# Fetching one gather chunk of every 7th block row by row on SyncE, instead of every 14th

## The reference, cut to what matters

```python
# layer 0: messages
h_nodes = mlp2(x, ...)                                   # per node
msgs = mlp2(concat(h_nodes[dst], h_nodes[src], h_edges)) # per edge
x = x + layernorm(x + upd(segment_mean(msgs, dst)))      # per node
# layer 1: attention, 4 heads of 32
h = x @ W
alpha = segment_softmax(leaky_relu(a_src[src] + a_dst[dst]), dst)
out = x + segment_sum(h[src] * alpha, dst) + bias
```

## Time and profile before

| | us |
|---|---|
| median of 3 runs | 4091.2 (4089.45 to 4092.23) |
| the profiled execution | 4091.22 |
| its span, first to last instruction | 4089.1 |
| GpSimd busy | 2965.8 (73%) |
| PE busy | 3382.9 (83%) |
| first and last gather of the message pass start at | 112.1 and 2056.0 |
| first and last gather of attention start at | 2109.8 and 4053.1 |

### The profile page before, as it was taken

The page is one execution under the profiler, slowest core; times in us unless marked ns, Lnnn a source line. Parts: engine busy times, 40 slices in busy tenths (PEclk is TensorE's granted clock), DMA queues, the critical chain, the costliest instruction groups (busy, mean ns, idle before and its releaser), DMA issues. The chain is left out here.

```text
span 4089.1 us, 126775 instructions
## 1 busy us (share of the span) xinstructions
PE 3382.9 (83%) x30848; PEld 2976.2 (73%) x30849; DVE 2517.0 (62%) x10511; ACT 2850.5 (70%) x5940; POOL 2965.8 (73%) x3134
## 2 busy tenths in 40 slices
PE   7789888999988899999947777777777778777777
PEld 4677777777777788888847777777777767766776
DVE  5752222222222256777748777777777777888888
ACT  6466565656556577788738777777777777877777
POOL 2677777777777777777737777777777777777774
PEclk8789999999899899999967777777777777777777
DMA  5322222222222233333342222222222222332332
GB/s 159 88 60 53 54 55 53 56 53 53 55 54 53 60 83 91 91 96 95 81 120 58 57 58 58 57 58 58 58 57 58 58 58 63 79 78 76 78 78 58
DMA packets 319769, 282.90 MB, mean 69 GB/s; under 512 B 143418, under 2 KB 242924, under 8 KB 319532
## 3 DMA queue, kind: packets, MB, share of 16 engines
q0 software_dynamic: 99456, 159.33, 15.9%
q1 hardware_dynamic: 139224, 79.62, 7.4%
q10 hardware_dynamic: 80852, 41.75, 3.5%
HBM read 249.58 MB, written 29.40 MB: 68 GB/s over the span
## 5 line engine op out<-in xcount | busy, mean ns | idle before, releaser
L541 POOL DMA_INDIRECT a_G<-Htab,idx x1554 | 1470.8, 946 | 526.3 <-issue 464.0
L541 POOL DMA_INDIRECT p_rows<-Btab,idx x1554 | 1471.4, 947 | 475.1 <-issue 473.4
L1799 PE MATMUL a_psA<-a_GP,a_S 128*128 128x132 f32 x4704 | 892.5, 365 | 2.7 <-DVE a_GP L1634 2.7
L1799 PEld LDWEIGHTS a_psA<-a_GP,a_S 128*128 128x128 f32 x4704 | 821.5, 268 | 8.2 <-DVE a_GP L1634 3.1
L1056 DVE TENSOR_TENSOR p_z<-p_psZ,p_rows 128x512 f32<-128x512 f32 x294 | 195.9, 689 | 829.4 <-SPq L746 679.6
L1206 ACT COPY p_ST<-p_psT 128x1024 bf16<-128x1024 bf16 x294 | 300.5, 1022 | 563.7 <-PE p_psT L1318 543.4
L1730 ACT CAST a_S<-a_Sb 128x512 f32<-128x512 bf16 x588 | 608.6, 1144 | 0.0
L1365 PE MATMUL p_psA<-p_msg,p_S 128*128 128x65 f32 x4704 | 589.9, 284 | 10.9 <-ACT p_S L1227 9.8
L1365 PEld LDWEIGHTS p_psA<-p_msg,p_S 128*128 128x128 f32 x4704 | 571.6, 201 | 16.5 <-issue 12.8
L1227 ACT CAST p_S<-p_Sb 128x1024 f32 (+1 forms) x294 | 582.6, 1982 | 0.0
L1341 PEld LDWEIGHTS p_psZ<-wc,p_s 128*128 128x128 f32 x2352 | 325.1, 206 | 204.7 <-issue 103.5
(11 more groups left out here) (212 smaller groups left out, 5165.8 us busy)
## 6 DMA issues: line engine op xcount, KB each, us to landing
arena<-in_ea SPq DMA_DIRECT2D x196, 256.0 KB
p_single<-Btab SPq DMA_DIRECT2D x1792, 0.2 KB
a_single<-Htab SPq DMA_DIRECT2D x1792, 0.5 KB
p_rows<-Btab,idx POOLq DMA_INDIRECT x1554
a_G<-Htab,idx POOLq DMA_INDIRECT x1554
Htab<-u_H ACTq DMA_DIRECT2D x49, 136.0 KB
arena<-Htab SPq DMA_DIRECT2D x7, 952.0 KB
n_x<-in_x SPq DMA_DIRECT2D x14, 448.0 KB, 4.0
```

The source lines that it names most:

```text
L541: pool.indirect_dma_start(out=rows[:, u * C + c, :], out_offset=None, in_=table, in_offset=bass.IndirectOffsetOnAxis(ap=idx[u][:, c:c + 1] ...
L1799: m = pe.matmul(psA[v][:, 0:HR], S32[v][:, c, :], GP[v][:, c, :], start=c == 0, stop=c == C - 1)
```

## The change

SyncE takes the eighth chunk of the last block of every round of 7 blocks, the first round excepted, instead of every 14. That makes 27 such chunks in each pass instead of 14. GpSimd issues 7 x 28 x 8 - 27 = 1,541 indirect DMAs in each pass instead of 1,554. The row DMAs of SyncE go from 1,792 to 3,456 in each pass. They are fetched one round ahead into a doubled spare tile, in seven batches of 12, 20, 20, 20, 20, 16 and 20 rows, one after each block's `ready`.

The node numbers are turned into byte offsets once, in the opening: ACT loads them, DVE multiplies them by 256 and by 544, and SyncE stores both tables to HBM (`offsets`). The row DMA then reads a flat byte view of the table at the offset in the register. The source indices of GpSimd come as one DMA for 7 blocks, no longer as one DMA for each block. The tile `flagt` moves onto the storage of `x1`, with one wait on DVE at row NORM.

```diff
-BATCH = (12, 12, 12, 8, 12, 8, 12, 8, 12, 8, 12, 12)
+BATCH = (12, 20, 20, 20, 20, 16, 20)
+ROUNDS = NB // SLOTS
...
+            sp.wait_ge(s_off, 18)
+            for n in range(2):
+                sp.dma_start(offsets[n], bytes_[n][:, :]).then_inc(s_off, 16)
+            sp.wait_ge(s_off, 50)
...
+            act.dma_start(nodes[:, :], t["single"]).then_inc(s_off, 16)
...
+                dve.wait_ge(s_off, 16)
+                for n, size in enumerate((4 * H, 4 * HROW)):
+                    dve.tensor_scalar(bytes_[n][:, :], nodes[:, :], size, None, ALU.mult).then_inc(s_off, 1)
...
-        for c in range(C - 1 if odd and u == SLOTS - 1 else C):
+        for c in range(C if whole or u < SLOTS - 1 else C - 1):
+            at = u * C + c
             pool.indirect_dma_start(
-                out=rows[:, u * C + c, :], out_offset=None, in_=table,
-                in_offset=bass.IndirectOffsetOnAxis(ap=idx[u][:, c:c + 1], axis=0)).then_inc(s_g[u], 16)
+                out=rows[:, at, :], out_offset=None, in_=table,
+                in_offset=bass.IndirectOffsetOnAxis(ap=idx[odd][:, at:at + 1], axis=0)).then_inc(s_g[u], 16)
...
+        at = self.nc.values_load_multi_w_load_instructions(
+            self.k["at"][0:1, odd * P + first:odd * P + first + BATCH[n]], engines=[sp.engine], min_val=0,
+            max_val=(NP - 1) * self.size, skip_runtime_bounds_check_because="offsets of nodes")[1]
         for p in range(BATCH[n]):
-            sp.dma_start(self.spare[first + p:first + p + 1, :], self.table[bass.ds(which[p], 1), :]
-                         ).then_inc(self.s_row[n % 3], 16)
+            sp.dma_start(self.spare[first + p:first + p + 1, odd, :].bitcast(U8),
+                         self.table[bass.ds(at[p], self.size)].unsqueeze(0)).then_inc(self.s_row[n % 6], 16)
...
+    def landed(self, i):
+        for n in range(6):
+            self.sp.wait_ge(self.s_row[n], 16 * sum(BATCH[n::6]) * (i + self.before))
+            self.sp.sem_inc(self.s_turn, 1)
+
+    def step(self, i, odd, u, first, final):
+        if not first and u == 0:
+            self.landed(i)
+        if not first and u == SLOTS - 2:
+            self.place(i, odd)
+        if not final:
+            self.batch(i + 1, 1 - odd, u)
+            if u == 0 and not (isinstance(i, int) and i + 2 >= ROUNDS):
+                self.load(i + 2, odd)
...
-            load_idx(u if final else (i + 1) * SLOTS + u, u)
-            step_singles(singles, r, odd * SLOTS + u, final)
+            if u == 0:
+                load_idx(sp, t, k, 0 if final else i + 1, 1 - odd)
+            singles.step(i, odd, u, first, final)
```

More of the change, by code:

```diff
@@ L63 @@
 BOUNDED = "build_steps cuts blocks and windows off at their last"
-assert W == NG * GW and NG % 2 == 0 and NS % 2 == 0 and NB % SPAN == 0 and sum(BATCH) == P and len(BATCH) < SPAN
+assert W == NG * GW and NG % 2 == 0 and NS % 2 == 0 and NB % SPAN == 0 and sum(BATCH) == P and len(BATCH) == SLOTS
 assert 2 * MEAN - 6 >= NB - 1 and 2 * MEAN - 201 + 195 >= NB
@@ L138, in build @@
         k["mcur"], k["adst"] = k["attn"][:, :, 0:NH], k["attn"][:, :, NH:2 * NH]
[L141 to L145, removed]
+        k["at"] = sb("at", [1, 2 * P], I32)
+        k["singles"] = [sem("at"), [sem(f"row{n}") for n in range(6)], sem("to")]
+        k["slots"] = [[sem(f"src{u}") for u in range(2)]] + [[sem(f"{n}{u}") for u in range(SLOTS)] for n in ("rows", "side")]
+        k["idx"] = [sb(f"idx{u}", [P, SLOTS * C], I32) for u in range(2)]
         with ExitStack() as ctx:
-            opening(nc, t, k, hTkeep, Btab, lambda *a: sb(*a, ctx=ctx), sem, ctx)
+            opening(nc, t, k, hTkeep, Btab, offsets, lambda *a: sb(*a, ctx=ctx), sem, ctx)
         with ExitStack() as ctx:
-            message_pass(nc, t, k, Btab, Htab, hTkeep, x1keep, flagrows, lambda *a: sb(*a, ctx=ctx), sem, ctx)
+            message_pass(nc, t, k, Btab, Htab, hTkeep, x1keep, flagrows, offsets, lambda *a: sb(*a, ctx=ctx), sem, ctx)
         with ExitStack() as ctx:
-            attention_pass(nc, t, k, Htab, flagrows, x1keep, out, lambda *a: sb(*a, ctx=ctx), sem, ctx)
+            attention_pass(nc, t, k, Htab, flagrows, offsets, x1keep, out, lambda *a: sb(*a, ctx=ctx), sem, ctx)
 def moments(dve, s_link, link, x, bn, mv, s_turn):
@@ L233, in opening @@
     s1 = sb("n_s1", [H, GW * P])
+    nodes, bytes_ = sb("nodes", [ROUNDS, P], I32), [sb(f"bytes{n}", [ROUNDS, P], I32) for n in range(2)]
+    s_off = sem("c_off")
     psT, psU, psV = (ctx.enter_context(nc.psum_tensor(f"n_ps{n}", [P, 2, 512], F32)) for n in "TUV")
@@ L532, in gather_blocks, with block @@
     s_idx, s_g, _ = k["slots"]
-    def block(i, odd, u, used):
-        if due(16 * (i + 1 + turns)):
-            pool.wait_ge(s_idx[u], 16 * (i + 1 + turns))
+    def block(r, odd, u, used, whole=False):
+        if u == 0:
+            pool.wait_ge(s_idx[odd], 16 * (r + 1 + turns // 2))
         if used is not None:
@@ L549, in gather_blocks @@
     for u in range(SLOTS):
-        block(0, False, u, None)
+        block(0, 0, u, None, whole=True)
     if s_table is not None:
@@ L554, in gather_blocks @@
     for u in range(SLOTS):
-        block(1, True, u, used[u])
-    with pool.Fori(1, NB // SPAN) as r:
+        block(0, 1, u, used[u])
+    with pool.Fori(1, ROUNDS // 2) as r:
         used = used_by(r * SPAN, SPAN)
@@ L559, in gather_blocks, with __init__ @@
             for u in range(SLOTS):
-                block(2 * r + odd, odd == 1, u, used[odd * SLOTS + u])
+                block(r, odd, u, used[odd * SLOTS + u])
 class Rows:
-    def __init__(self, nc, sp, t, k, table, spare, at, to, s_used, s_turn, turn):
-        self.nc, self.sp, self.t, self.k, self.table, self.spare, self.at, self.to = nc, sp, t, k, table, spare, at, to
-        self.s_used, self.s_turn, self.turn = s_used, s_turn, turn
+    def __init__(self, nc, sp, k, table, offsets, spare, to, s_used, s_turn, turn):
+        self.nc, self.sp, self.k, self.offsets, self.spare, self.to = nc, sp, k, offsets, spare, to
+        self.size = 4 * table.shape[1]
+        self.table = table.rearrange("n f -> (n f)").bitcast(U8)
+        self.s_used, self.s_turn = s_used, s_turn
@@ L569, in __init__, with load, batch @@
         self.s_at, self.s_row, self.s_to = k["singles"]
[L570 to L575, removed]
+        self.before = (ROUNDS - 1) * turn
+    def load(self, i, odd):
+        self.sp.dma_start(self.k["at"][0:1, odd * P:(odd + 1) * P], self.offsets[bass.ds(i, 1), :]).then_inc(self.s_at, 16)
+    def batch(self, i, odd, n):
         sp, first = self.sp, sum(BATCH[:n])
@@ L591, in place @@
             skip_runtime_bounds_check_because=BOUNDED)[1][0]
-        for n in range(3):
-            sp.wait_ge(self.s_row[n], 16 * sum(BATCH[n::3]) * (r + 1 + self.total))
-            sp.sem_inc(self.s_turn, 1)
         sp.wait_ge(self.s_used, used)
         sp.sem_inc(self.s_turn, 1)
-        sp.dma_start(self.to, self.spare[:, :]).then_inc(self.s_to, 16)
-    def placed(self, r):
-        self.sp.wait_ge(self.s_to, 16 * (r + 1 + self.total))
+        sp.dma_start(self.to, self.spare[:, odd, :]).then_inc(self.s_to, 16)
@@ L601, in placed @@
+    def placed(self, i):
+        self.sp.wait_ge(self.s_to, 16 * (i + self.before))
         self.sp.sem_inc(self.s_turn, 1)
-def gathers(r, odd, u, turns):
-    if u < SLOTS - 1:
[L607 to L618, removed]
@@ new lines, in step, with gathers @@
+    def step(self, i, odd, u, first, final):
[7 more added lines that the diff above has]
+                self.load(i + 2, odd)
+def gathers(i, u, turns):
+    if u < SLOTS - 1:
+        return 16 * C * (i + 1 + turns)
+    return (16 * (C + (C - 1) * (turns - 1)) if turns else 0) + 16 * (C - 1) * i + 16 * C
@@ L633, in arrived, with load_idx, feed_blocks @@
+def load_idx(sp, t, k, i, odd):
+    sp.dma_start(k["idx"][odd][:, :], t["src"].rearrange("(i p) c -> i p c", p=P)[bass.ds(i, 1)]
+                 .rearrange("o p c -> (o p) c")).then_inc(k["slots"][0][odd], 16)
+def feed_blocks(nc, sp, t, s_used, s_turn, s_ready, k, side, turns, then, singles):
+    _, s_g, s_side = k["slots"]
+    def arrived(i, u):
+        sp.wait_ge(s_g[u], gathers(i, u, turns))
         sp.sem_inc(s_turn, 1)
@@ L639, in feed_blocks @@
         side(u, u)
-    singles.load(0)
+    singles.load(1, 1)
     then()
@@ L645, in blocks @@
         for u in range(SLOTS):
[L646 to L650, removed]
+            if u == SLOTS - 1 and not first:
+                singles.placed(i)
+            arrived(i, u)
+            if u == 0 and not final:
+                load_idx(sp, t, k, i + 1, 1 - odd)
             if not (final if u >= SLOTS - 2 else first):
@@ L661, in used_at @@
             skip_runtime_bounds_check_because=BOUNDED)[1]
-    last = NB // SPAN - 1
+    last = ROUNDS // 2 - 1
     blocks(0, 0, first=True)
@@ L705, in run_rows, with feed_messages @@
         body(row, valid, updates)
[L708 to L715, removed]
```

(18 more changed lines are left out.)

42 lines of the change are left out of this document (17 added, 25 removed).

## The result

The changed kernel takes 4067.76 us (median of 5 runs, 4062.53 to 4070.66), the kernel before beside it 4091.2 us (5 runs). The ratio is 0.9941, with a 95% interval of 0.9930 to 0.9951: 20 to 29 us less. 4061.5 us was forecast, with a range of 4056 to 4078. The profiled execution is the fastest of the five, 4062.53 us with a span of 4060.8 us.

The account below looks back on a forecast made before the run. GpSimd's unbroken gather issue was taken as the bound; 14.2 us off messages, 16.2 off attention and 0.7 added in the opening gave -29.7 us from 4091.2, so 4061.5 us, range 4056 to 4078.

Parts of the forecast that it names:

- The bound: Both passes: GpSimd issues gathers without a break, 1.2475 us each; 14 blocks go from 138.6 to 137.4 us.
- attention's share: Attention, bound by POOL from end to end: 13 fewer gathers at 1.2475 us count in full, 16.2 us.
- The message pass: Messages: 9 gathers before the node update count in full, 4 in it count 3 of 5.0 us; 14.2 us.
- The prediction's own sign: DVE's wait for SyncE's word (L746) stays large before 1400 us and vanishes in the node update.
- The part before the update: Messages before the node update: 9 of 13 saved gathers fall there, 11.2 us counted in full.
- rival C: Node update: compute takes all of the 5 us (4059.5) or none (4064.5); inside the forecast's range, no separate chance.
- The FUSED_REGOPS: SyncE's row DMA: byte offsets remove the index multiplication and its gap, 0.08 us a row, 0.42 to 0.34 us.
- Its work: SyncE's sum in 14 blocks: 131 us in messages, 134 in attention, under GpSimd's 137.4 with 6 and 3 spare.
- The opening: Before the passes: SyncE issues two more DMAs after the last Btab store; bounds 0 and 2.7 us, 0.7 taken.
- The sum: Whole kernel: -14.2 messages, -16.2 attention, +0.7 opening, together -29.7 us, giving 4061.5 us.
- Rival A: SyncE becomes the bound: FUSED_REGOPS stays (+350 us, 4440) or loads of 20 cost 4.7 us (+870, 4960); 15 in 100.
- The skill's rule: SyncE's register loads at about 200 ns a register: 256 values 51 us, not 20, making SyncE the bound in both passes.

Follow-up runs that it names:

- fewer_gathers: The changed kernel with one gather fewer in each of 27 rounds of the message pass; 4044.09 us, ratio 0.9883 to the kernel before.
- after_again: The changed kernel run once more, unaltered, on another comparison chip; 4069.86 us, ratio 0.9931 to the kernel before.

## Why the prediction was right, and where its sum was off

*The bound.* Right. GpSimd's pitch, its 137.4 us for 14 blocks and attention's share (16.2 forecast, 16.7 measured) are as read from the earlier trace rows.

*The message pass.* The mechanism, a gather counts only while GpSimd is the bound, was right, and one term was mis-sized: "Bounds: nothing, and 5.0 us. DVE still waited 38 us in this stretch, some of which can be used, and I take 3." By the table 0.2 us came back, nothing within the scatter. The 38 us could not be used: with GpSimd some 18 us further ahead of the last read than before (fewer_gathers), the stretch lasted as long. Where these waits lie could be read before. 24.1 of the 31.2 us fall into 1430 to 1500 us, its first 70:

```profile
DVE p_z L1056 <- SPq L746: 24.1, 4, 9.6
```

There the readers still waited for GpSimd's rows, gap by gap. After 1500 us PE is busy for 95 to 98% and four loop rows take 53.1 us with nothing to wait for the earlier trace rows. That it is PE that holds the readers is read from these shares; no run made the compute shorter. The prediction's own sign, that DVE's wait for SyncE vanishes in the update, did not come: it stayed at 38.2 us. The part before the update gave 10.0 us where 11.2 was forecast. Messages: 14.2 forecast, 10.0 measured. This is rival C's end, 4064.5 us.

*SyncE.* The FUSED_REGOPS went, as argued from the earlier trace rows, and takes 0.09 us a row with its gaps, not 0.08. A row takes 0.324 us (0.34 forecast), a load of 20 takes 1.36 us (1.53). Its work is 126 and 128 us where 131 and 134 were summed: 256 rows at 0.016 us less and ten loads at 0.17 less account for it. It had 11 and 10 us free, where 6 and 3 were forecast.

*The opening.* 0.7 us was taken of 0 to 2.7. In the changed kernel SyncE issues the two stores behind the last `Btab` store and has the next pass's index DMA out 2.6 us after that store's issue ends; before it was 2.56 us (109.76 - 102.12 - 5.08). Nothing, then. First the rows of before, then those of the changed kernel:

```profile
102.12 5.08 SPq L283 DMA_DIRECT2D Btab<-n_b  x2
109.76 3.50 SPq L714 DMA_DIRECT2D idx<-in_src  x7
...
97.37 5.09 SPq L288 DMA_DIRECT2D Btab<-n_b  x2
102.51 0.98 SPq L301 DMA_DIRECT2D offsets<-bytes  x2
105.07 0.38 SPq L641 DMA_DIRECT2D idx<-in_src  x1
```

*The sum* with the measured terms is -10.0 - 16.7 = -26.7 us, 4064.5 us. The median is 3 us above it; the comparison on this chip gave 23.4 us, after_again's 29.2, and 26.7 lies between. That the profiled execution took 4062.53 us, 1 us from the forecast, is luck: its message pass gained only 7.4 us, and 4.9 us came from the opening's scatter.

*Rival A.* Its two causes were built and both made the kernel slower, by 6.3% and 9.5%. The prices were too high: 350 us forecast for the returned FUSED_REGOPS, 259 measured, since the round came to 149 us and not 151 and 154, and since not every one of the 13 rounds paid in full. For the loads it took 4.7 us for 20 values, 870 us in all; they take 4.25, and the kernel built, 390 us slower, has only five of its seven loads off a multiple of four.

*The skill's rule.* The Trainium skill, "Runtime: NRT & Kernel Launch", section "Instruction fetch mechanics", gives about 200 ns for each register loaded. The runs agree for loads that begin off a multiple of four (4.25 / 20 = 0.21 us) and not for those that begin at one (1.36 / 20 = 0.068 us). The loads here read SBUF; no run loads from HBM. Had the rule held for the loads that begin at one, SyncE would have been the bound: 256 x 0.2 = 51 us by the page's figure instead of 18 puts its round, as an estimate, at 126 + 33 = 159 us.

## What to carry to other kernels

Work taken off the bounding engine is worth its full price only in the stretches where that engine is the bound: cut the pass at the place where another engine comes level, and count nothing behind it. Small waits that the readers still show there may lie at its start, so look where they fall before a part of them is taken as gain. When work moves to a queue engine, sum that engine's whole round, not only the moved DMAs; here two details of 0.09 us a row and 2.9 us a load decided between 0.6% faster and 6 to 10% slower. A small excess of the queue engine over the bound is paid in nearly every round (rounds of 149 us against 137 made 13 such rounds a pass 6% slower).

## What the runs showed of the hardware that was not expected

A register load of SyncE from SBUF costs 1.36 us for 20 values when it begins at a multiple of four values of its tile, and 4.25 or 4.24 us when it begins one or two past it. Seven values cost 1.12 us at a multiple of four and 1.64 us at one, two and three past it. No start gave a value between: wherever a load of seven begins off a multiple of four, it takes the same time.

The kernel before took 4092 and 4099 us on two chips and 6944 us on a third. There GpSimd's gathers had the same median of 944 ns:

```profile
L541 POOL DMA_INDIRECT p_rows<-Btab,idx x1554: 938/944/2789, 109.1 to 3373.4; - x195
```

But the gaps before them with nothing visible to wait for sum to 3,714 us, where they are 937 us in the first profile. What stopped the engines is not shown.
